# Recurrences in 96 dense rows: 16 half-width passes a line, seeds on ScalarE, row copies on VectorE

## The reference

```
x = x + attention(group_norm(x))
x = x + recurrences(group_norm(x))

step(w, b): next = line + conv1d(state, w, b)     # 48 -> 48 channels, 5 taps, padding 2
D: down the rows,    step(down_w, down_b)
U: up the rows of D, step(down_w, down_b)
R: right over the columns of U, step(right_w, right_b)
L: left over the columns of R,  step(left_w, left_b)
```

## Time and profile before

| | before |
|---|---|
| median of 3 runs | 10179.8 us |
| profiled execution | 10184.16 us |
| its span, first to last instruction | 10182.5 us |
| mean granted TensorE clock | 0.957 |
| TensorE / VectorE / ScalarE / GpSimd busy | 9178.7 / 6163.4 / 6540.9 / 2811.9 us |
| attention | 0 to about 5060 us |
| the four recurrences | 5093 to 9443 us |
| final sum | from 9443 us |

### The profile page before, as it was taken

One profiled execution on the slowest core, in us unless ns is written; L12 is line 12 of the kernel. 1 busy time (PEld: TensorE's weight loads), 2 busy tenths in 40 slices (PEclk: granted clock), 3 DMA queues, 4 the chain that ended last, 5 costly groups with the idle time before them and its releaser, 6 DMA issues. The chain is left out here.

```text
span 10182.5 us, 167735 instructions
## 1 busy us (share of the span) xinstructions
PE 9178.7 (90%) x53872; PEld 7753.5 (76%) x53872; DVE 6163.4 (61%) x10420; ACT 6540.9 (64%) x10026; POOL 2811.9 (28%) x2287
## 2 busy tenths in 40 slices
PE   3999999999999999999899999999999999999000
PEld 3999999999999998777677777777777777777000
DVE  8888888777777775666633335666433336666323
ACT  2777777777777775444377777888877775555000
POOL 0000000000000000000156665666566656666000
PEclk9999999999999999999999999999999999999555
DMA  8888887666666665999989986777766657777999
GB/s 268 171 166 170 170 169 145 129 132 131 134 135 132 133 135 132 291 291 287 257 182 206 198 206 184 218 218 217 206 223 212 220 180 203 203 202 190 371 433 408
DMA packets 770594, 2101.18 MB, mean 206 GB/s; under 512 B 58976, under 2 KB 633728, under 8 KB 674256
## 3 DMA queue, kind: packets, MB, share of 16 engines
q1 hardware_dynamic: 629824, 1744.21, 67.0%
q0 software_dynamic: 34304, 151.01, 5.8%
q10 hardware_dynamic: 106368, 204.76, 5.6%
HBM read 1344.55 MB, written 754.97 MB: 206 GB/s over the span
## 5 line engine op out<-in xcount | busy, mean ns | idle before, releaser
L1483 DVE TENSOR_TENSOR lo<-scan_ps,hi 112x512 fp32r<-112x512 f32 x2048 | 1416.1, 691 | 2263.0 <-PE scan_ps L1414 1130.7
L1588 ACT CAST hi<-scan_ps 112x512 fp32r<-112x512 f32 x2048 | 1202.9, 587 | 1095.5 <-PE scan_ps L1401 1082.7
L463 PE MATMUL conv_ps<-tap_low,x_high 128*128 128x432 f32 (+2 forms) x6144 | 1904.9, 310 | 0.0
L463 PE MATMUL conv_ps<-tap_high,x_low 128*128 128x432 f32 (+2 forms) x6144 | 1903.6, 310 | 0.0
L463 PE MATMUL conv_ps<-tap_high,x_high 128*128 128x432 f32 (+2 forms) x6144 | 1881.0, 306 | 13.0 <-DVE x_edge L659 7.5
L1401 PE MATMUL scan_ps<-hi,scan_high 112*112 112x512 f32 x6132 | 1777.4, 398 | 40.4 <-ACT hi L1588 33.0
L1414 PE MATMUL scan_ps<-lo,scan_high 112*112 112x512 f32 x6132 | 1769.8, 397 | 0.6
L1409 PE MATMUL scan_ps<-hi,scan_low 112*112 112x512 f32 x6132 | 1768.2, 397 | 0.0
L1520 POOL TENSOR_TENSOR lines<-hi,lo 112x512 f32<-112x512 f32 x1024 | 1323.0, 1292 | 871.4 <-DVE lo L1483 871.4
L1520 POOL TENSOR_TENSOR ring<-hi,lo 112x512 f32<-112x512 f32 x1024 | 1326.2, 1295 | 843.9 <-DVE lo L1483 843.9
L1401 PEld LDWEIGHTS scan_ps<-hi,scan_high 112*112 112x112 f32 x6132 | 1075.4, 176 | 408.6 <-ACT scan_ps L1567 18.0
(11 more groups left out here) (145 smaller groups left out, 11670.0 us busy)
## 6 DMA issues: line engine op xcount, KB each, us to landing
raw<-x SPq DMA_DIRECT2D x764, 256.0 KB, 4.9
d_rows<-lines SPq DMA_DIRECT2D x32, 3584.0 KB, 24.3
u_cols<-lines SPq DMA_DIRECT2D x64, 1792.0 KB, 10.6
r_cols<-lines SPq DMA_DIRECT2D x32, 3584.0 KB, 16.6
lines<-u_cols SPq DMA_DIRECT2D x31, 3584.0 KB, 16.4
lines<-r_cols SPq DMA_DIRECT2D x30, 3584.0 KB, 16.6
lines<-d_rows SPq DMA_DIRECT2D x30, 3360.0 KB, 15.5
v_blocks<-xs ACTq DMA_DIRECT2D x128, 768.0 KB, 4.5
```

The source lines that it names most:

```text
L463: nc.tensor.matmul(bank(dy, side, lo - side, hi - side), xs[at], ws[taps], start=fresh[side], stop=False, skip_group_check=True)
L1483: nc.vector.tensor_tensor(low_of(k), ps[:, k % SLOTS], high_of(k), ALU.subtract).then_inc(lo_ready, 1)
L1588: nc.scalar.copy(high_of(k), ps[:, k % SLOTS]).then_inc(hi_ready, 1)
```

## The change

The two sets of 48 channels move together, to partitions 0 to 95 (`SC` = 96), and the 256 pairs of positions of a line are parted again into even pairs (`X`) and odd pairs (`Y`) of 128 each. A pass can now be of one half: 2 images x 128 = 256 columns. Of a set of taps, only 4 of the 6 shifts by one pair have half-wide passes whose source lies in the other half; a line has 1 pass of 512 columns and 14 of 256 (16 half-widths) in place of 9 of 512.

The free partitions 96 to 127 of `hi` and `lo` get copies of 32 rows of the `Y` half of `hi`, and the free rows of the tap matrices the low taps that belong to them, so that passes over all 128 rows do part of a further pass. VectorE makes these three copies in every line, before its `lo`; TensorE's low products wait for the first of them (`high_spare`), and for the others through `lo_ready`.

All seeds are set by ScalarE, two lines ahead, also in "up" and "left". The ring is gone: GpSimd writes the turned state itself, with steps (`state`), and waits for the tile's earlier store. PSUM has 8 banks for lines. In "down" the loads of the second 48 rows are issued by ScalarE's queue, and SyncE issues the next loads when `hi` is through with a group rather than when its seeds are. "up" is stored by four DMAs instead of two. The memset of partitions 32 to 63 is gone.

```diff
+    d_rows = dram("d_rows", (G, SC, T, B * W2))
+    u_cols = dram("u_cols", (G, 2, C, 2, G, NP * 2 * B * N))
+    r_cols = dram("r_cols", (G, SC, T, B * W2))
...
+                        rows, spare = slice(0, SC), slice(SC, 128)
+                        nc.vector.tensor_copy(scan_high[rows, :, 3], scan_taps[:, :, 1])
+                        link(nc.vector.tensor_copy(scan_high[rows, :, 0:3], scan_taps[:]))
+                        link(nc.vector.tensor_tensor(scan_low[rows], scan_taps[:], scan_high[rows, :, 0:3], ALU.subtract))
+
+                        for tile, at, first, shift in ((scan_low, 0, 32, 1), (scan_low, 1, 32, 2), (scan_high, 0, 64, 1),
+                                                       (scan_high, 1, 64, 2), (scan_high, 2, 0, 2), (scan_high, 3, 0, 1)):
+                            nc.vector.tensor_copy(tile[spare, :, at], scan_low[first:first + 32, :, shift])
...
-    LP = W2
-    RING = 16
-    LEAD = 4
+    LQ = W2 // 2
+    ROWS, SPARE = slice(0, SC), slice(SC, 128)
+    X, Y = 0, 1
     LAG = 2
     ACT_AHEAD = 2
-    DVE_AHEAD = 3
-    HIS, LOS, SLOTS = 4, 2, 4
+    HIS, LOS, SLOTS = 4, 2, 8
...
-    STORES = {"down": 1, "up": 2, "right": 1, "left": 4}
+    STORES = {"down": 1, "up": 4, "right": 1, "left": 4}
...
+        lines = [sb(f"lines{n}", [SC, 2, T * B * W2]) for n in range(2)]
+        skipped = sb("skipped", [SC, B * W2])
+        hi = sb("hi", [128, HIS, 2, B, LQ + 2], F32R)
+        lo = sb("lo", [128, LOS, 2, B, LQ + 2], F32R)
...
+        banks = ctx.enter_context(nc.psum_tensor("scan_ps", [PP, SLOTS, 2, B, LQ], F32))
+        ps = banks[ROWS]
...
+                q, x, m = k % 2, k // 2 % 2, k // 4
+                tile = arriving(way, s).rearrange("p (q u j y x b m) -> p q y b (u j) x m", q=2, u=G, j=4, y=2, x=2, b=B)
+                return tile[:, q, :, :, :, x, m]
...
...
         def high_of(k):
-            return hi[:, k % HIS, :, 1:LP + 1]
+            return hi[ROWS, k % HIS, :, :, 1:LQ + 1]
 
         def low_of(k):
-            return lo[:, k % LOS, :, 1:LP + 1]
+            return lo[ROWS, k % LOS, :, :, 1:LQ + 1]
+
+        def spare_of(tile, x):
+            return tile[SPARE, x, :, 1:LQ + 1]
+
+        def odd_rows(k, at):
+            return hi[at:at + 128 - SC, k % HIS, Y, :, 1:LQ + 1]
...
+                    sp.wait_ge(hi_ready, states0(way) + T * g - T)
+
+                def written(way, g):
+                    sp.wait_ge(state_done, states0(way) + T * g + T)
...
-                def slot(k):
-                    return ps[:, k % SLOTS]
+                def half(way, k, x, taps, at, of, x_in, shift, rows=ROWS):
+
+                    return nc.tensor.matmul(ps[:, k % SLOTS, x], taps[rows, TAPS_OF[way], at], of[rows, x_in, :, shift:shift + LQ],
+                                            start=False, stop=False, skip_group_check=True)
 
                 def high_products(way, g, k):
 
-                    pe.wait_ge(seeded[way], seeds0(way) + T * g + k + 1)
+                    high = hi[:, (k - 1) % HIS]
+                    pe.wait_ge(seeded[way], T * g + k + 1)
                     pe.wait_ge(hi_ready, states0(way) + T * g + k)
-                    for shift in range(3):
-                        last = nc.tensor.matmul(slot(k), w_hi[:, TAPS_OF[way], shift], hi[:, (k - 1) % HIS, :, shift:shift + LP],
-                                                start=False, stop=False, skip_group_check=True)
-                    last.then_inc(conv_done, 1)
+                    nc.tensor.matmul(ps[:, k % SLOTS], w_hi[ROWS, TAPS_OF[way], 1], high[ROWS, :, :, 1:LQ + 1],
+                                     start=False, stop=False, skip_group_check=True)
+                    half(way, k, X, w_hi, 0, high, Y, 0)
+                    half(way, k, Y, w_hi, 0, high, X, 1)
+                    half(way, k, X, w_hi, 2, high, Y, 1)
+                    half(way, k, Y, w_hi, 2, high, X, 2).then_inc(conv_done, 1)
 
                 def low_products(way, g, k):
 
+                    high, low, every = hi[:, (k - 1) % HIS], lo[:, (k - 1) % LOS], slice(0, 128)
                     pe.wait_ge(hi_ready, states0(way) + T * g + k + 1)
-                    for shift in range(3):
-                        nc.tensor.matmul(slot(k), w_lo[:, TAPS_OF[way], shift], hi[:, (k - 1) % HIS, :, shift:shift + LP],
-                                         start=False, stop=False, skip_group_check=True)
+                    pe.wait_ge(high_spare, states0(way) + T * g + k)
+                    half(way, k, Y, w_lo, 0, high, X, 1, every)
+                    half(way, k, X, w_lo, 0, high, Y, 0)
+                    half(way, k, X, w_lo, 1, high, X, 1, every)
+                    half(way, k, Y, w_lo, 2, high, X, 2)
 
                     pe.wait_ge(lo_ready, states0(way) + T * g + k)
-                    for shift in range(3):
-                        last = nc.tensor.matmul(slot(k), w_hi[:, TAPS_OF[way], shift], lo[:, (k - 1) % LOS, :, shift:shift + LP],
-                                                start=False, stop=shift == 2, skip_group_check=True)
-                    last.then_inc(low_done, 1)
+                    half(way, k, Y, w_hi, 0, low, X, 1, every)
+                    half(way, k, X, w_hi, 0, low, Y, 0)
+                    half(way, k, X, w_hi, 1, low, X, 1, every)
+                    half(way, k, Y, w_hi, 3, low, Y, 1, every)
+                    half(way, k, X, w_hi, 2, low, Y, 1, every)
+                    half(way, k, Y, w_hi, 2, low, X, 2).then_inc(low_done, 1)
...
                 def steps(way, g, first=False, last=False):
                     for k in range(2 * T):
                         done = states0(way) + T * g + k
                         v.wait_ge(hi_ready, done + 1)
+                        nc.vector.tensor_copy(spare_of(hi[:, k % HIS], X), odd_rows(k, 32)).then_inc(high_spare, 1)
+                        nc.vector.tensor_copy(spare_of(lo[:, k % LOS], Y), odd_rows(k, 0))
+                        nc.vector.tensor_copy(spare_of(lo[:, k % LOS], X), odd_rows(k, 64))
                         if not (first and k == 0):
                             v.wait_ge(low_done, convs0(way) + T * g + k)
                         if not (way == "down" and first and k < LOS):
                             v.wait_ge(state_done, done - LOS + 1)
                         nc.vector.tensor_tensor(low_of(k), ps[:, k % SLOTS], high_of(k), ALU.subtract).then_inc(lo_ready, 1)
-                        if way in laid:
-                            ahead = k + DVE_AHEAD
-                            if ahead < 2 * T:
-                                seed(way, g + ahead // T, ahead // T, ahead, first)
-                            elif not last:
-                                seed(way, g + ahead // T, ahead // T - 2, ahead - 2 * T)
...
+                def state(way, s, k):
+
+                    high, low = high_of(k), low_of(k)
+                    if way == "up":
+                        r, h = (T - 1 - k % T) % 2, (T - 1 - k % T) // 2
+                        tile = leaving(way, s).rearrange("p (r c h x b m) -> p r h (x b) c m", r=2, c=W // T, h=NP, x=2, b=B)
+                        return (tile[:, r, h], high.rearrange("p x b (c m) -> p (x b) c m", c=W // T),
+                                low.rearrange("p x b (c m) -> p (x b) c m", c=W // T))
+                    if way == "left":
+                        tile = leaving(way, s).rearrange("p (b m x t) -> p x b m t", b=B, x=2, t=T)
+                        return tile[..., T - 1 - k % T], high, low
+                    return leaving(way, s).rearrange("p (t x b m) -> p t x b m", t=T, x=2, b=B)[:, k % T], high, low
...
-                        nc.gpsimd.tensor_tensor(state(way, s, k), high_of(k), low_of(k), ALU.add).then_inc(state_done, 1)
+                        to, high, low = state(way, s, k)
+                        nc.gpsimd.tensor_tensor(to, high, low, ALU.add).then_inc(state_done, 1)
...
+                        if way == "down" and k == LAG and not first:
+                            act.wait_ge(seeded[way], T * g)
+                            load_down(act, g + 1, 1, 1)
+                        if way == "down" and k == T + LAG and not last:
+                            act.wait_ge(seeded[way], T * g + T)
+                            load_down(act, g + 2, 0, 1)
+                        ahead = k + ACT_AHEAD
+                        if ahead < 2 * T:
+                            seed(way, g + ahead // T, ahead // T, ahead, first)
+                        elif not last:
+                            seed(way, g + ahead // T, ahead // T - 2, ahead - 2 * T)
```

More of the change, by code:

```diff
@@ L24 @@
 PP = ODD + C
+SC = 2 * C
 T = 16
@@ L1186, in scans @@
         hi_ready, state_done, lo_ready = sem("hi_ready"), sem("state_done"), sem("lo_ready")
-        act_seeded, dve_seeded = sem("act_seeded"), sem("dve_seeded")
-        seeded = {"down": act_seeded, "up": dve_seeded, "right": act_seeded, "left": dve_seeded}
+        seeded = {way: sem(f"{way}_seeded") for way in WAYS}
```

(38 more changed lines are left out.)

182 lines of the change are left out of this document (61 added, 121 removed).

## The result

| | before | after |
|---|---|---|
| median | 10180.4 us (10179.8 to 10181.5) | 11232.6 us (11223.8 to 11237.7, 4 runs) |
| profiled execution, its span | 10184.2, 10182.5 us | 11223.8, 11222.2 us |
| mean granted TensorE clock | 0.957 | 0.962 |
| first and last `lo` of the recurrences start | 5095.1, 9443.3 us | 5090.2, 10486.4 us |

The change makes the kernel slower: ratio 1.103, interval 1.101 to 1.105. 11,385 us had been predicted. The recurrences, from the first `lo` to the last, take 5396.2 us in place of 4348.2: 1048 us more, against 1040 between the two profiled executions. A line in the timeline takes 2.62 us in place of 2.11, and (2.62 - 2.11) x 2044 = 1042 us.

A forecast was written before the change was run, and what follows sets the result against it. TensorE's streamed columns bound the kernel before, 2.11 us a line; lo, sum and copies in series were to take 2.70. 10184 + 1206 = 11390, as a median 11,385 us; 8-in-10 range 9,820 to 12,200.

The forecast's parts named there:

- The main case: In each recurrence line, lo, GpSimd's sum and VectorE's three copies run in series: 2.70 us, 11,385 us; chance 50%.
- Sums and copies exclude each other: VectorE's SBUF-to-SBUF copies and GpSimd's sum cannot run together; they share 2.15 us in every recurrence line.
- The sum gets in between the first and the second copy: GpSimd's sum starts when the first copy ends, at 0.20 to 0.29 us; the second copy waits for it.
- The size of the line: lo 0.69, sum 1.29 and copies 0.86 make 2.84 us, less three overlaps of 0.08: 2.60; 2.70 taken.
- TensorE's passes: 14 passes of 256 columns at 0.120 us and one of 512 take 1.91 us a line (1.77 to 2.10).
- rival 3: TensorE's half passes run at a weight load's pace, the line stays 2.10 us: 10,170 us; chance 3%.
- ScalarE: Cast and seeds a line: 1.33 us in up and left, 1.75 in right, 1.54 to 2.02 in down.
- DMA and queues: Loads, stores and issues in the recurrences cost nothing under a longer line; late loads up to 90 us over down.
- GpSimd's stepped writes: Sums written with steps in up and left stay at 1.29 us; at 2.2 us, up to +930 us.
- The clock: TensorE keeps full clock in the recurrences despite 0.8 us idle a line; at 1.2 GHz, 1.91 us becomes 3.8.
- Rival 2: Copies and GpSimd's sum run side by side, TensorE bounds the line at 1.91 us: 9,830 us; chance 21%.
- Rival 1: The three copies go together ahead of GpSimd's sum, line 2.16 us: 10,286 us (10,060 to 10,560); chance 26%.

The follow-up runs named there:

- the mix: Changed kernel with the first copy kept and the second and third made additions of PSUM zeros: 9826.9 us, ratio 0.965 to the kernel before.

## Why the prediction was right

The main case happened, by its mechanism: one copy long, two short, `lo` ending TensorE's idle time, ScalarE and TensorE beneath. Step by step:

- **Sums and copies exclude each other.** Right, and shown from both sides: additions of the same rows with an operand in PSUM run beside the sum at their own length, and copies added to the old layout are held up as in the new. The memset of the earlier trace rows stood rightly for a sum.
- **The sum gets in between the first and the second copy.** Right. Making it wait for the third gives 2.14 us a line instead of 2.62. By the letter of one of the signs given ("if GpSimd's sums and the copies overlap in the timeline") the forecast would be wrong, since the records overlap: the sum starts 0.18 us before the first copy ends. The long second copy shows that the rest excludes.
- **The size of the line.** 2.70 was forecast, 2.62 measured, and this term alone makes the error: 0.08 x 2044 = 164 us, where 11,385 - 11,233 = 152 were missed. The sum of the parts was 2.84 before overlaps. Two places were not seen. The sum starts 0.18 us before the first copy is over and gets only about 0.04 longer (means of 1321 to 1333 ns where it meets the end of a copy, 1291 to 1298 where it doesn't). And the held second copy ends 0.15 after the sum, not 0.29: half of its length isn't held. So the long copy has a mean of 1.27 us and not the near 1.5 that was forecast. Together 0.28 us. The three overlaps of 0.08 that the prediction did take off don't exist: `lo` to copy is +0.03, copy to copy +0.01 to +0.03, copy to `lo` +0.01; with the joints 2.84 - 0.28 + 0.06 = 2.62. The choice of 2.70 between 2.60 and 2.84 was a middle of two sums, one of which had wrong parts and nearly the right total: that 2.60 lies so near 2.62 is luck.
- **TensorE's passes.** 1.91 forecast; 1.92 measured where nothing covers it. The four half passes that make up 0.64 us of the timeline lie (0.64 - 0.28) / 3 = 0.12 us apart. The earlier trace rows bounded this well, and rival 3 is out.
- **ScalarE.** Contiguous seeds 690 ns (0.74 forecast), columns in "right" 1180 (1161), and the two activations of "down" 575 against 567: reading every second word costs next to nothing, so the upper bound of 2.02 us fell. ScalarE is beneath TensorE's time in all four ways but for its DMA issues.
- **DMA and queues.** Costed at nothing under a longer line, which holds: the loads and stores fit. The issues on ScalarE's queue, put at 0.06 us a line if uncovered, cost 12.6 to 14 us over "down" in kernels whose line is 1.92, about 0.03 a line.
- **GpSimd's stepped writes.** Taken at nothing, right: all 2048 sums are in one group of mean 1327 ns, and in the kernel without copies the mean is 1298, against 1.29 for the row. The bound of 2.2 us fell.
- **The clock.** Taken full, right: 1.00 granted in the recurrences in spite of 0.46 us of idle time a line, but for some 10 us at each turn (0.50 from 6436 to 6442 us, at the 1.2 GHz level, behind idle times of 1.17 and 4.91 us). The reason given had a row wrong: there are no gaps of 2.2 us between the first lines of the kernel before. TensorE had stood idle 17.30 us before its first high products at 5095.22, and then once more for 0.77 us. So "a third of the latter" compares with nothing that the trace has, and that the clock held is luck as far as that reason goes.
- **Rival 2**, the side on which the forecast would have been wrong, was put at 9,830 us. The kernel without copies took 9,813 and the mix 9,827. Its mechanism is false for copies; its price was right.
- **Rival 1's lower end** doesn't follow from its line: 1.98 us would be 9,918 us, and 10,060 stands for 2.05. It changed nothing, as the line of that run, 2.14 us, is above both.

The Trainium skill, page "VectorE: DVE Perf Modes", section "Two Vector instructions with no wait between them", has a rule that would have avoided the false overlaps: an instruction of which an operand starts in another group of 32 partitions than in the last instruction that read (or, for its output, wrote) the same memory starts only when the earlier ones are over. The traces agree as far as they go. `lo` and seed, all from partition 0, overlap by 0.08; every joint with a copy, which reads or writes at another start than its neighbour, has a gap of 0.01 to 0.03 us. No run varied the start alone, so that this is the cause isn't shown.

## What to carry to other kernels

Before work is given to VectorE, look at what kind it is and not only at its idle time: an SBUF-to-SBUF copy of 0.29 us cost 0.39 us a line because it had to wait out GpSimd's 1.29 us beside it. If copies and GpSimd's work together exceed the bound, make a copy an addition with zeros in PSUM (0.43 us, beside the sum at full speed), and only as many of them as must be: the first copy, which starts ahead of the sum, was free. Look for equal instructions of unequal length: here one of three equal copies had four times the mean of the others, because it waited inside its own duration, which VectorE's busy share counted as work.

## What the runs showed of the hardware

- A held copy ends 0.14 to 0.17 us after GpSimd's sum (5302.57 after 5302.42, 6803.53 after 6803.39, 6800.92 after 6800.77, 6802.55 after 6802.38), though it takes 0.29 alone. The sum, too, can start 0.18 us before a copy ends for 0.04 us more. Whether that part is fetch and set-up ahead of the exclusive part, or the records' ends, can't be told from these traces.
- The right was handed over at each instruction: with two sums back to back, a copy was let in after each of them, and the two sums still started 1.27 us apart (6801.08 and 6802.35).
- With more idle time the clock did fall. In the kernel with two sums TensorE was busy two thirds of the recurrences, and the granted clock was 0.90 there and 0.913 over the span. In one line of it four half passes took 1.05 us instead of 0.64, behind an idle time of 1.46 us; in the line before, behind 1.44 us, they took 0.64. Both lines are 3.6 us long, since the slower passes are still covered. In the kernel after, with 0.46 us idle in 2.62, they take 0.64, and the granted clock of the recurrences is 1.00.
- The memset of the earlier trace rows had held the statistics' small copy for 6.90 us. It is gone with the change, and the same copy takes 0.17 us in the trace after.
